# A routed expert stage whose TensorE program is written out slot by slot, in place of a hardware loop

## The chip, the cores and the metric

The kernel runs on one core of a Trainium2 chip. The metric is the device time of one execution in microseconds (us). A core has five engines with instruction streams of their own: TensorE (PE: matmuls, with the weight loads shown as PEld), VectorE (DVE), ScalarE (ACT), GpSimd (POOL) and SyncE (SP). They meet through semaphores. Sixteen DMA engines move data between HBM and SBUF.

## The reference

Three blocks over 4096 rows (2 sequences of 2048) of 256 numbers, all in fp32. The middle block is a state space layer; the first and the last are the same feed-forward layer with a shared expert and eight routed ones:

```python
x = x + 0.5 * ffn(layernorm(x), ...)
x = x + attn(layernorm(x), ...)      # x @ W_in, causal conv, 16-state recurrence, silu, @ W_out
x = x + 0.5 * ffn(layernorm(x), ...) # the same weights as the first

def swiglu(x, wg, wu, wd):
    return silu(x @ wg.T) * (x @ wu.T) @ wd.T

def ffn(h, gate_w, shared_gate, shared_up, shared_down, r_gate, r_up, r_down):
    shared_out = swiglu(h, shared_gate, shared_up, shared_down)
    logits = h @ gate_w.T
    top_id = argmax(logits, axis=-1)
    xs = h * sigmoid(max(logits, axis=-1))[:, None]
    routed_out = 0
    for e in range(8):
        xe = where((top_id == e)[:, None], xs, 0.0)
        routed_out += swiglu(xe, r_gate[e], r_up[e], r_down[e])
    return shared_out + routed_out
```

## The kernel before

**Layout.** fp32 matmuls are made of three passes over operands that are split into a high and a low part (`mm3`, lines 350 to 352: high by high, low by high, high by low). The feed-forward layer is in the program twice, called layer 0 (first block) and layer 1 (third block). Each has this order on TensorE: the shared expert on the first half of the rows, then the routed stage, then the shared expert on the second half.

**Routed stage.** The rows are scattered by expert into `xs_sorted` in HBM, in 39 slots of 128 rows (32 tiles, and up to 7 more since each expert's rows end on a slot's edge). The slots are worked in order, in 13 rounds of `RING` = 3. Which expert a slot belongs to is known only when the kernel runs: DVE writes it into the table `slot_e`, and TensorE reads one entry into a register (`expert_of`, line 537; `TENSOR_LOAD` in the trace). The register's lowest bit picks one of two places of the expert's weights, `wr_hi` and `wr_lo`.

**One slot on TensorE** (`routed_run`, from line 540): 12 matmuls for gate and up of slot s (`m_gate_up`, columns 512), the read of the next slot's expert, 2 transposes of the rows of slot s + 1 (`m_transpose`, line 501), 12 matmuls for down of slot s - 1 (`m_down`, columns 256), and 4 transposes of the hidden rows of slot s (`m_transpose_h`, line 532). ACT and DVE take the results over in between, and SP loads and stores slots (`slot_load`, line 1618; `slot_store`, line 1622).

**Pieces.** `routed_run` is called in pieces. Layer by layer, slots 0 to 2 are written out; a hardware loop of 3 turns holds the code of 9 slots (slots 3 to 11, 12 to 20, 21 to 29); slots 30 to 38 are written out again. Every piece but the first begins with two reads of the table, one for the slot before it and one for its first slot, because nothing is carried over from the piece before. Inside a piece only the following slot is read, in mid-slot. In the loop, the slot number and the semaphore values that are waited for are computed in registers. ACT, DVE and SP have loops of their own over rounds of 3 slots.

**Weights.** POOL loads each expert's weights twice, into `wr_raw` (line 1452) and `wr_hi` (line 1455), 1536 KB each, and subtracts one from the other into `wr_lo` (line 1471, 6.8 us). It starts the load of `wr_hi` of an expert when TensorE has finished the slots of the expert two before it, and that of `wr_raw` as soon as the subtraction before is done.

Of the kernel before, what the change touches and what calls it, by code (L numbers as in the profile page):

```python
# [30 lines left out]
def build(nc, x, w_routed, w_shared, gate_w, w_in, w_out, vecs, b_in, b_out, ssm_a, ssm_bc, ssm_d, out):  # L31
# [19 lines left out]
    NS = NT + E - 1  # L51
    RING = 3
# [19 lines left out]
    with ExitStack() as ctx:  # L72
# [283 lines left out]
        def _(pe):  # L356
# [140 lines left out]
            def m_transpose(L, s, j, use):  # L497

                pe.wait_ge(s_xsl[j], 16 * (L * (NS // RING) + use + 1))
                for kb in range(KB):  # L500
                    mm = pe.transpose(MXT[:, kb * P:(kb + 1) * P], rows[:, j, kb * P:(kb + 1) * P],  # L501
                                      ident[:, :])
                mm.then_inc(s_mt, 1)

            def m_gate_up(L, s, e, par):
                q = L * NS + s
                pe.wait_ge(s_wl, e + (L * E + 1))
                pe.wait_ge(s_mxl, q + 1)
                for o, c0, done in ((MG, 0, s_mg), (MU, UP0, s_mu)):
                    for kb in range(KB):  # L510
                        cs = par * W + (c0 + kb * F)
                        wh = wr_hi[:, :, :].rearrange("p a w -> p (a w)")[:, bass.ds(cs, F)]
                        wl = wr_lo[:, :, :].rearrange("p a w -> p (a w)")[:, bass.ds(cs, F)]
                        mm = mm3(pe, o[:, :], xT_hi[:, kb, 0:P], xT_lo[:, kb, 0:P], wh, wl,
                                 start=(kb == 0), stop=(kb == KB - 1))
                    mm.then_inc(done, 1)

            def m_down(L, s, par):
                q = L * NS + s
                pe.wait_ge(s_mhl, q + 1)  # L520
                for fb in range(FB):
                    cs = par * W + (DN0 + fb * H)
                    wh = wr_hi[:, :, :].rearrange("p a w -> p (a w)")[:, bass.ds(cs, H)]
                    wl = wr_lo[:, :, :].rearrange("p a w -> p (a w)")[:, bass.ds(cs, H)]
                    mm = mm3(pe, MY[:, 0:H], hT_hi[:, fb, 0:P], hT_lo[:, fb, 0:P], wh, wl,
                             start=(fb == 0), stop=(fb == FB - 1))
                mm.then_inc(s_slot, 1)

            def m_transpose_h(L, s):
                pe.wait_ge(s_mh, L * NS + s + 1)  # L530
                for fb in range(FB):
                    mm = pe.transpose(MHT[:, fb * P:(fb + 1) * P], hf[:, 0, fb * P:(fb + 1) * P],  # L532
                                      ident[:, :])
                mm.then_inc(s_mth, 1)

            def expert_of(s):
                e = pe.value_load(slot_e[0:1, bass.ds(s, 1)], min_val=0, max_val=E - 1)
                return e, e % 2

            def routed_run(L, i0, count, first=False, last=False):  # L540

                prev = None if first else expert_of(i0 * RING - 1)[1]
                now = expert_of(i0 * RING)
                for a in range(count):
                    for j in range(RING):
                        i, s = i0 + a, (i0 + a) * RING + j
                        end = a == count - 1 and j == RING - 1
                        m_gate_up(L, s, *now)
                        following = None if end else expert_of(s + 1)
                        if not (last and end):  # L550
                            m_transpose(L, s + 1, (j + 1) % RING, i + (j + 1) // RING)
                        if prev is not None:
                            m_down(L, s - 1, prev)
                        m_transpose_h(L, s)
                        prev, now = now[1], following
                if last:
                    m_down(L, (i0 + count) * RING - 1, prev)

            def routed_slots(L):
                pe.wait_ge(s_tab, L + 1)  # L560
                pe.wait_ge(s_add, 2 * (L * NG + NH))
                m_transpose(L, 0, 0, 0)
                routed_run(L, 0, 1, first=True)

                rounds, each = NS // RING - 1, 3
                loops = (rounds - 1) // each
                with pe.Fori(0, loops) as h:
                    routed_run(L, each * h + 1, each)
                routed_run(L, loops * each + 1, rounds - loops * each, last=True)

            def w_in_sums():

# [130 lines left out]
            pe.wait_ge(s_wsl, 1)  # L703
            shared(0, 0)
            routed_slots(0)
            shared(0, 1)
            attention()
            shared(1, 0)
            routed_slots(1)
            shared(1, 1)  # L710

# [1042 lines left out]
```

## Time and profile before

| | us |
|---|---|
| median of 3 runs | 957.38 |
| lowest and highest of them | 955.56, 959.16 |
| the profiled execution, its own time | 956.44 |
| span in its trace | 954.3 |
| TensorE busy, all matmuls | 893.9 |
| routed stage of layer 0, slots 0 to 38 | 153.4 to 355.2 |
| routed stage of layer 1, slots 0 to 38 | 677.8 to 876.5 |

All times in the trace are counted from the start of the span. The profiled execution took 956.44 us, 2.1 us more than its span; it lies 0.9 us under the median. A matmul's end is modelled, and matmuls overlap, so the starts are the safe numbers: the distance from the first gate matmul of one slot to that of the next is the slot's period. Idle time called "issue" is time in which TensorE waited for nothing that the profile shows. Register instructions and branches do not count as busy; they appear under PEldq, TensorE's sequencer.

### The profile page before, as it was taken

Reading aid. Unit: us, or ns where it says so; the run is one execution under the profiler, and the core shown is the slowest. Engines: PE = TensorE matmul, PEld = TensorE weight load, DVE = VectorE, ACT = ScalarE, POOL = GpSimd, SP = SyncE. Lnnn points to the kernel's source line nnn. Section 1 sums busy time; section 2 is a strip of 40 time slices with the busy share of each in tenths; the row PEclk is TensorE's granted clock in tenths of the full one; section 3 lists DMA queues with packets and bytes.
Section 4 is the critical chain, followed back from the end, with each engine's and each line's share of the span. In section 5 each row is a group of like instructions: output and inputs, shape, how many; then the busy total and the mean of one; then the engine's idle time right before and its main releaser. Section 6 shows DMA issues by size and latency. Waiting matters only on the chain.

```text
span 954.3 us, 16363 instructions
## 1 busy us (share of the span) xinstructions
PE 893.9 (94%) x5430; PEld 784.7 (82%) x5431; DVE 476.3 (50%) x1007; ACT 383.2 (40%) x747; POOL 459.1 (48%) x427
## 2 busy tenths in 40 slices
PE   4899998999999999998999997999899999998998
PEld 3788887888888888887989997888788888887887
DVE  6447553333333335558998983755333333333453
ACT  1134232333333333346677765423233333333331
POOL 3314764124242207864999985376431242220883
PEclk9999999999999999999999998799999999999999
DMA  8836564355555316520011104646434555511557
GB/s 279 285 122 235 161 242 166 111 188 177 185 182 180 100 39 149 72 29 1 12 29 29 45 23 143 201 164 244 165 124 177 185 187 176 188 56 57 93 101 182
DMA packets 75676, 130.85 MB, mean 137 GB/s; under 512 B 6650, under 2 KB 67716, under 8 KB 71268
## 3 DMA queue, kind: packets, MB, share of 16 engines
q0 software_dynamic: 18688, 74.33, 25.2%
q1 hardware_dynamic: 56932, 55.75, 18.4%
q8 instruction: 38, 0.62, 0.3%
q14 instruction: 18, 0.15, 0.1%
HBM read 93.74 MB, written 36.32 MB: 136 GB/s over the span
## 4 chain that ended last, share of the span: by engine, by line
PE 70%; DMA 11%; DVE 7%; POOL 5%; issue 4%; ACT 1%; SPq 1%; POOLq 0%; ACTq 0%; DVEq 0%
PE bank L350 19%; PE bank L352 18%; PE bank L351 18%; DMA rows<-xs_sorted 9%; PE bank L425 4%; PE bank L417 3%; PE bank L532 3%; PE bank L501 2%; DMA xs_sorted<-rows,pos 1%; DVE v L1164 1%; POOL v L1410 1%; POOL xs_sorted L1438 1%; DMA rows<-xn_kept 1%; POOL hT_lo L1414 1%; DVE xT_lo L945 1%
## 5 line engine op out<-in xcount | busy, mean ns | idle before, releaser
L350 PE MATMUL bank<-wr_hi,xT_hi 128*128 x312 | 130.4, 418 | 9.9 <-issue 7.5
L1471 POOL TENSOR_TENSOR wr_lo<-wr_raw,wr_hi 128x3072 fp32r<-128x3072 f32 x14 | 95.1, 6795 | 87.0 <-DMA wr_hi<-w_routed 86.9
L1495 POOL DMA_INDIRECT acc<-ys_sorted,pos x64 | 102.2, 1597 | 62.4 <-DMA ys_sorted<-rows 41.2
L352 PE MATMUL bank<-wr_lo,xT_hi 128*128 x312 | 123.9, 397 | 0.0
L351 PE MATMUL bank<-wr_hi,xT_lo 128*128 x312 | 123.7, 396 | 0.0
L1121 DVE TENSOR_TENSOR hf<-sg,bank 128x512 f32<-128x512 f32 x78 | 53.6, 687 | 135.7 <-PE bank L352 135.7
L945 DVE TENSOR_TENSOR hT_lo<-bank,hT_hi 128x512 fp32r<-128x512 f32 x78 | 54.0, 692 | 125.7 <-ACT hT_hi L716 125.7
L350 PE MATMUL bank<-xT_hi,ws_hi 128*128 128x512 f32 x256 | 102.3, 400 | 3.9 <-DVE xT_lo L945 2.7
L351 PE MATMUL bank<-xT_hi,ws_lo 128*128 128x512 f32 x256 | 101.6, 397 | 0.0
L716 ACT ACTIVATE xT_hi<-bank 128x256 fp32r<-128x256 f32 (+1 forms) x126 | 56.0, 463 | 112.8 <-PE bank L501 96.0
L352 PE MATMUL bank<-xT_lo,ws_hi 128*128 128x512 f32 x256 | 101.2, 395 | 0.0
L732 ACT ACTIVATE sg<-bank 128x512 f32<-128x512 f32 x64 | 38.3, 598 | 154.4 <-PE bank L352 154.3
L350 PE MATMUL bank<-wr_hi,hT_hi 128*128 x312 | 94.3, 302 | 3.0 <-DVE hT_lo L945 3.0
L352 PE MATMUL bank<-wr_lo,hT_hi 128*128 x312 | 88.1, 282 | 0.0
L351 PE MATMUL bank<-wr_hi,hT_lo 128*128 x312 | 87.8, 281 | 0.0
L1043 DVE TENSOR_TENSOR hf<-sg,bank 128x512 f32<-128x512 f32 x64 | 43.8, 687 | 76.5 <-PE bank L352 76.2
L1438 POOL DMA_INDIRECT xs_sorted<-rows,pos x64 | 64.8, 1013 | 35.7 <-DVE rows L1083 17.9
L350 PEld LDWEIGHTS bank<-wr_hi,xT_hi 128*128 128x128 f32 x312 | 59.3, 190 | 23.0 <-issue 12.4
L780 ACT ACTIVATE sg<-bank 128x512 f32<-128x512 f32 x78 | 46.6, 597 | 77.0 <-PE bank L352 77.0
L1164 DVE SCALAR_TENSOR_TENSOR v<-bank,vec,v 128x511 f32<-128x511 f32 (+2 forms) x96 | 71.0, 747 | 7.5 <-ACT v L849 5.0
L1455 POOL DMA_DIRECT2D wr_hi<-w_routed x16 | 8.9, 555 | 136.0 <-PE bank L352 136.0
L350 PE MATMUL bank<-ws_hi,hT_hi 128*128 128x256 f32 x256 | 73.5, 287 | 0.0
(236 smaller groups left out, 2265.2 us busy)
## 6 DMA issues: line engine op xcount, KB each, us to landing
wr_raw<-w_routed POOLq DMA_DIRECT2D x16, 1536.0 KB, 7.0
wr_hi<-w_routed POOLq DMA_DIRECT2D x16, 1536.0 KB, 7.8
rows<-xs_sorted SPq DMA_DIRECT2D x78, 128.0 KB, 2.4
ys_sorted<-rows SPq DMA_DIRECT2D x78, 128.0 KB, 1.7
xn_kept<-xg SPq DMA_DIRECT2D x16, 512.0 KB, 3.3
xg<-xn_kept SPq DMA_DIRECT2D x16, 512.0 KB, 4.3
rows<-xn_kept SPq DMA_DIRECT2D x16, 512.0 KB, 4.1
acc<-x SPq DMA_DIRECT2D x8, 512.0 KB, 7.4
```

The lines of the kernel that those rows point to most:

```text
L350: pe.matmul(o, a_hi, b_hi, start=start, stop=False, skip_group_check=True)
L351: pe.matmul(o, a_lo, b_hi, start=False, stop=False, skip_group_check=True)
L352: return pe.matmul(o, a_hi, b_lo, start=False, stop=stop, skip_group_check=True)
L716: return act.activation(o, i, ACT.Copy)
L780: act.activation(sg[:, 0, :], MG[:, :], ACT.Silu).then_inc(s_msg, 1)
L945: return dve.tensor_tensor(o, full, f32(h), ALU.subtract)
L1043: dve.tensor_tensor(hf[:, fb % 2, :], sg[:, fb % 2, :], U2[fb % 2][:, :], ALU.mult).then_inc(s_h, 1)
L1121: dve.tensor_tensor(hf[:, 0, :], sg[:, 0, :], MU[:, :], ALU.mult).then_inc(s_mh, 1)
L1164: dve.scalar_tensor_tensor(vb_[:, d:GN], UB[cb % 2][:, 0:GN - d], vec[:, cb, k:k + 1], vb_[:, d:GN], ALU.mult, ALU.add).then_inc(s_tap if ...
L1438: pool.indirect_dma_start(out=xs_dram, out_offset=bass.IndirectOffsetOnAxis(ap=pos[:, tt:tt + 1], axis=0), in_=rows[:, half * GT + t, :], ...
L1471: pool.tensor_tensor(wr_lo[:, e % 2, :], wr_raw[:, :], f32(wr_hi[:, e % 2, :]), ALU.subtract).then_inc(s_wl, 1)
L1495: pool.indirect_dma_start(out=acc[:, tt, :], out_offset=None, in_=ys_dram, in_offset=bass.IndirectOffsetOnAxis(ap=pos[:, tt:tt + 1], axis= ...
```

## The change

On TensorE, the four pieces of the routed stage (three calls of `routed_run`, one of them in a loop) become one call that writes out all 39 slots. The table is read once for each slot, and what was read is carried on. All slot numbers and semaphore values are constants. The order of matmuls and of what they wait for is unchanged. The other engines' programs are the same. TensorE's program grows from 4476 to 6032 rows (both layers, waits left out, a matmul with its weight load as one row).

```diff
@@ -560,13 +560,7 @@
                 pe.wait_ge(s_tab, L + 1)
                 pe.wait_ge(s_add, 2 * (L * NG + NH))
                 m_transpose(L, 0, 0, 0)
-                routed_run(L, 0, 1, first=True)
-
-                rounds, each = NS // RING - 1, 3
-                loops = (rounds - 1) // each
-                with pe.Fori(0, loops) as h:
-                    routed_run(L, each * h + 1, each)
-                routed_run(L, loops * each + 1, rounds - loops * each, last=True)
+                routed_run(L, 0, NS // RING, first=True, last=True)
 
             def w_in_sums():
```

The places that move are the seams between the pieces: one where the loop is entered (between slots 2 and 3), two where it returns, one where it is left (between slots 29 and 30), in each layer. L567 is the line of the loop, `slot_e` the table, `m_h_done` the semaphore of the hidden rows. Here is TensorE's program before, in layer 0, from the last transposes of slot 2 to the first wait of slot 3:

```order
L532 MATMUL bank<-ident,hf 128x128 [waits m_h_done]
L532 MATMUL bank<-ident,hf 128x128 x3
L567 UNCONDITIONAL_BRANCH
L567 ISA
L537 REGISTER_ALU
L537 TENSOR_LOAD slot_e
L537 ISA x3
L537 TENSOR_LOAD slot_e
L537 ISA x2
L507 REGISTER_ALU
L508 REGISTER_ALU [waits wr_lo_done]
L350 ISA [waits m_xT_lo_done]
```

In the changed kernel the same place, and every other edge between slots, reads so:

```order
L532 MATMUL bank<-ident,hf 128x128 [waits m_h_done]
L532 MATMUL bank<-ident,hf 128x128 x3
L507 REGISTER_ALU
L350 ISA [waits m_xT_lo_done,wr_lo_done]
L350 MATMUL bank<-wr_hi,xT_hi 128x512
```

The branch, both reads and their register work are gone from between the transposes and the next slot's first matmul. The second place is the end of the loop's code in layer 0 and the start of the written-out slots 30 to 38, before:

```order
L532 MATMUL bank<-ident,hf 128x128 [waits m_h_done]
L532 MATMUL bank<-ident,hf 128x128 x3
L567 REGISTER_ALU
L567 COMPARE_AND_BRANCH
L537 TENSOR_LOAD slot_e
L537 ISA x2
L537 TENSOR_LOAD slot_e
L537 ISA x2
L507 REGISTER_ALU
L350 ISA [waits m_xT_lo_done,wr_lo_done]
```

In the changed kernel this place too has the five rows of the fence above it. One read stays for each slot; it stands in mid-slot, behind the twelve gate and up matmuls, as it does inside the pieces before.

## Rows read from the trace of the kernel before

**Rows 1.** The page: the chain that ended last, shares of the span by engine
```profile
PE 70%; DMA 11%; DVE 7%; POOL 5%; issue 4%; ACT 1%; SPq 1%; POOLq 0%; ACTq 0%; DVEq 0%
```

**Rows 2.** Nine slots each: length, busy PE, PEld, DVE, ACT, POOL, PE clock, DMA
```profile
170.30:216.81 46.51, 44.52 (x271) 38.54 (x271) 15.84 (x28) 17.49 (x36) 11.94 (x5) 1.00 0.45 154
...
263.39:309.81 46.42, 44.56 (x270) 38.56 (x271) 15.20 (x27) 17.44 (x36) 15.22 (x7) 1.00 0.54 186
309.81:353.60 43.79, 43.78 (x268) 38.54 (x268) 15.09 (x26) 16.54 (x35) 5.44 (x4) 1.00 0.23 73
```

**Rows 3.** Timeline of TensorE: start, duration, instruction, idle time before it
```profile
174.84 0.60 PE L532 MATMUL bank<-ident,hf 128*128 128x128 f32 x4
175.19 0.48 PE L350 MATMUL bank<-wr_hi,xT_hi 128*128 x1
...
215.12 0.60 PE L532 MATMUL bank<-ident,hf 128*128 128x128 f32 x4
216.81 0.49 PE L350 MATMUL bank<-wr_hi,xT_hi 128*128 x1 [1.09 <-issue]
```

**Rows 4.** TensorE's waits, 160:352.5, then 682:874: total us, times, longest
```profile
PE bank L350 <- issue: 3.6, 4, 1.1
PE bank L501 <- DMA rows<-xs_sorted: 3.1, 6, 0.7
...
PE bank L350 <- issue: 3.9, 4, 1.1
PE bank L501 <- DMA rows<-xs_sorted: 0.9, 2, 0.5
```

**Rows 5.** TensorE's sequencer, lines 537 and 567: count, ns min/median/max
```profile
L537 PEldq TENSOR_LOAD <-slot_e x86: 296/302/498, 151.8 to 865.8; - x86
...
L567 PEldq COMPARE_BRANCH  x6: 83/218/235, 214.5 to 829.2; - x6
```

**Rows 6.** The chain of waits: start, us, a slot load behind a weight load
```profile
181.14 7.28 DMA rows<-xs_sorted
```

**Rows 7.** Timeline of POOL and TensorE around the last weight load of layer 1
```profile
825.60 0.55 POOL L1455 DMA_DIRECT2D wr_hi<-w_routed  x1 [9.48 <-PE bank L352]
833.28 6.80 POOL L1471 TENSOR_TENSOR wr_lo<-wr_raw,wr_hi 128x3072 fp32r<-128x3072 f32 x1 [7.13 <-DMA wr_hi<-w_routed]
...
831.15 0.49 PE L350 MATMUL bank<-wr_hi,xT_hi 128*128 x1 [0.83 <-issue]
...
834.05 0.38 PE L501 MATMUL bank<-ident,rows 128*128 128x128 f32 x2
```

**Rows 8.** Timeline of POOL: weight loads in layer 0, then in layer 1
```profile
220.43 0.55 POOL L1452 DMA_DIRECT2D wr_raw<-w_routed  x1 [0.30 <-POOL wr_lo L1471]
226.99 0.55 POOL L1455 DMA_DIRECT2D wr_hi<-w_routed  x1 [6.01 <-PE bank L352]
...
769.55 0.57 POOL L1452 DMA_DIRECT2D wr_raw<-w_routed  x1 [0.30 <-POOL wr_lo L1471]
774.84 0.55 POOL L1455 DMA_DIRECT2D wr_hi<-w_routed  x1 [4.72 <-PE bank L352]
```

**Rows 9.** DMA queues, packets, MB, share: 180.5:188.5, 216:310 (whole list), 310:356, whole span
```profile
q8 instruction: 1, 0.02, 0.9%
...
q0 software_dynamic: 1152, 12.58, 37.1%
q1 hardware_dynamic: 5184, 4.72, 15.7%
...
q8 instruction: 3, 0.05, 0.4%
...
q8 instruction: 38, 0.62, 0.3%
```

**Rows 10.** Slot 0 of layer 0 and of layer 1, columns as in rows 2
```profile
153.40:159.43 6.03, 5.40 (x18) 4.00 (x19) 1.02 (x2) 0.98 (x2) 0.83 (x2) 0.72 0.77 268
677.82:682.30 4.48, 3.85 (x18) 2.88 (x19) 1.02 (x2) 0.98 (x2) 1.38 (x2) 1.00 0.56 163
```

## The prediction, made before the changed kernel was run

> **What bounds the kernel now.** I began with the chain that ended last. TensorE holds 70% of it, and "issue", time in which nothing that the profile shows was waited for, holds 4% [rows 1]. So a gap on TensorE is worth its length, if what waits behind it moves along. Next came the stretches of nine slots in the routed stage of layer 0, cut at the edges of the pieces. The reader is to compare the length with the busy PE: the first and the third turn of the loop take 46.51 and 46.42 us, and the written-out slots 30 to 38 take 43.79 us for the same matmuls, with TensorE busy for 43.78 [rows 2]. 43.79 / 9 = 4.87 us is thus a slot's period with no gap, and a turn of the loop loses 2.6 to 2.7 us.
>
> The timeline shows where. Between two slots inside a piece the last transposes start at 174.84 and the next slot's first matmul at 175.19: 0.35 us, which is 0.25 less than the modelled 0.60 of the transposes. At a return of the loop the same two starts are 215.12 and 216.81, 1.69 us apart, with 1.09 us of idle "issue" between [rows 3]. So a seam costs its idle time and 0.25 us more: 1.69 - 0.35 = 1.34 = 1.09 + 0.25. The waits of TensorE give all of them: 4 idle times "issue" of 3.6 us in layer 0 and 4 of 3.9 us in layer 1 [rows 4], one for each seam and none elsewhere between slots. The other idle time in the stage is before the transposes of the next slot's rows, on the load of `rows` from `xs_sorted`: 3.1 us in 6 places and 0.9 us in 2 [rows 4]. It is not touched by the edit.
>
> ACT, DVE and SP return from loops of their own at every third slot. If those were the cause, the gap would stand at every third slot; it stands at the four seams only.
>
> **What the change removes.** At each seam TensorE's sequencer has the loop's branch, two reads of the table and register work to do after it has issued four short transposes, and only their 0.60 us of work covers that. A read takes 302 ns in the middle of 86, a compare and branch 218 ns in the middle of 6 [rows 5]. Two reads and a branch are 0.82 us, and register work takes the rest of what is seen. In mid-slot the same read is covered by the backlog of twelve matmuls in front of it, and costs nothing in slots 30 to 38: busy 43.78 of 43.79 [rows 2]. After the change each edge is of that kind, and the number of reads falls from 86 to 78.
>
> Sum: layer 0 loses 3.6 + 4 x 0.25 = 4.6 us, layer 1 loses 3.9 + 4 x 0.25 = 4.9 us. Together **9.5 us less**.
>
> Register arithmetic inside the loop's slots goes too. A bound on what it costs now: a turn is 46.5 us at most, less 43.8, less a seam of at most 1.34, less its share of the slot load waits (3.1 idle and 6 x 0.17 of overlap lost, over three turns, 1.4): nothing or 0.1 us a turn, under 0.5 us in both layers. I take zero, since it lies before matmuls that are already queued, and the lower end is zero as well.
>
> **What the change adds.** First, program text. 18 slots a layer that were turns of the loop are now fetched. In the 94 us from 216 to 310, inside the loop, the list of DMA queues has no instruction queue at all; in the 46 us of the written-out slots 30 to 38 and a little more it has 3 packets of 16 KB [rows 9]. At 2 to 3 packets for nine slots, 18 slots in each of two layers add 8 to 12 packets to the 38 of the whole execution. Their price in a straight line: the stretch with 3 packets has no gap, and the 8 us from 180.5, under a weight load, have one such packet and no idle "issue". I take zero; the upper end is the rival on code below.
>
> Second, **given back on slot loads**. A slot's rows are loaded one to two slots before they are transposed. Where such a load is issued right behind a weight load it takes 7.28 us [rows 6], and TensorE waits a little for it. Eleven of the twelve weight loads `wr_hi` have no seam between the issue of the slot load and its use, so their waits stay what they are. The twelfth has one. It is issued at 825.60 and the subtraction that waits for it starts at 833.28; the slot load behind it lands about then. TensorE uses those rows at 834.05, after a seam of 0.83 + 0.25 = 1.08 us [rows 7]. Without the seam it would come at 832.97 and wait until 833.28: **0.3 us** given back.
>
> Third, the weights. POOL loads `wr_raw` at a fixed distance behind its own work, and `wr_hi` when TensorE has finished an expert. Where a seam lies between, the distance shrinks. It is 226.99 - 220.43 = 6.56 us in one of two such places of layer 0, and becomes 5.2. Layer 1 has already a distance of 774.84 - 769.55 = 5.29 us [rows 8] with no longer wait after it. POOL's idle time before these loads, 6.01 and 4.72 us [rows 8], is also about how early the next expert's weights are ready; minus 1.34 it stays above 3 us, so TensorE does not start to wait for `wr_lo`. A slot load behind `wr_raw` may lose some tenths where it comes 1.3 us nearer to it: 0 to 0.3 us in each of three places. I take 0.1 us in all.
>
> So 9.5 - 0.3 - 0.1 = **9.1 us** less. What follows each stage (the shared expert's second half, the gathers, the attention block) starts from it and moves along whole: none of it has a fixed time of its own. The span becomes 954.3 - 9.1 = 945.2, the profiled execution 956.44 - 9.1 = 947.3. It lay 0.9 under the median, and the forecast goes by the median: 957.38 - 9.1 = **948.3 us**.
>
> **What the skill says of a seam.** In this trace a return costs 1.34 us, and no instruction packet is moved from 216 to 310, though the loop returns in there. The Trainium skill, in "Runtime: NRT & Kernel Launch", section "Instruction fetch mechanics", says that a taken branch whose target isn't in the current two-page window forces a fetch before work goes on; no run of before shows such a fetch at a return. By that rule the seam would be a fetch, and by the rows it is sequencer work; the sum is the same, as both go. The Trainium skill, in "Advanced Engine Details and Errata", section "Control Flow Timing", gives about 51 ns for a branch and 108 ns for a compare and branch; the trace has 218 ns for most of the latter. By that page alone the loop itself would be worth under 1 us over eight seams, an estimate, and the reads would have to be the rest.
>
> **The rivals.** (1) *Slot loads take part of the gain.* They are the only other idle time in the stage, and a faster TensorE needs them sooner. The longest wait now is 0.7 us [rows 4]. If all twelve loads behind a weight load came to wait so long, that is 8.4 us in place of the present 4.0: 4.4 us given back, 957.38 - 9.5 + 4.4 = 952.3 us. Against it: eleven are triggered by TensorE itself and keep their distance. Chance 0.08.
>
> (2) *The idle time is not the seam's.* Something at a slot's start that the trace doesn't name could hold it, as the register work in front of the first matmul, and the edge of a written-out slot could keep most of it. Then under 1 us changes, about 956.5 us. Against it: slots 31 to 38 have these very edges and no gap [rows 2]. Chance 0.04.
>
> (3) *Slower: code comes late.* The loop ran from code already on chip, and the new text is fetched in the same 94 us in which weights take 37.1% of the DMA engines' time [rows 9]. Suppose a packet is asked for only when it is needed. Of 10 added packets four would queue behind weights for up to the 7.3 us of a slot load there, and six cost about 1.3 us, the dearest seam as the nearest row for an unloaded fetch: 4 x 7.3 + 6 x 1.3 = 37 us, 985 us. It decides from 0.9 us a packet, where the gain is gone. Against it stand the packets in straight code that cost nothing, one of them under weights. Chance 0.04.
>
> Besides, TensorE's clock in slot 0 is 0.72 in layer 0 (part of it at 1.2 GHz) and 1.00 in layer 1, after a short idle time in both, and the slot takes 6.03 against 4.48 us [rows 10]. The two could change places or both go one way: 1.6 us up or down, whatever the change does.
>
> **How the numbers follow.** The forecast has 0.84. Around 948.3 lie the clock's 1.6 us, 0.5 for register work, 0.9 more for loads behind `wr_raw`, and the spread of the runs (1.8 us on either side of the median): 945.3 to 951.6. To leave out no more than 2 in 10, the upper end goes to rival (1): **945.0 to 952.5 us**. A measurement of this kernel can tell about 0.5% from no change, 4.8 us: faster means below 952.6. Faster 0.84 and most of (1)'s 0.08: 0.90. Within 0.5%: the rest of (1) and (2): 0.06. Slower 0.04.
>
> **What would show it.** Right: no idle "issue" before L350 between slots; 78 reads and no compare and branch; layer 0's stage down from 201.8 us by 4.6, layer 1's from 198.7 by 4.5; 46 to 50 instruction packets, some of them in the stretch that had none; slot load waits near 4 us in all with a new one of 0.3 in slot 30 of layer 1. Wrong: idle "issue" spread over the written-out slots at any place (code), the load waits of [rows 4] grown to 8 us (rival 1), or a gap left at every slot's start (rival 2).

## The result, and the profile of the changed kernel

The changed kernel takes **960.03 us** (median of 16 runs, 958.01 to 965.39), the kernel before 957.39 us on the same chip (16 runs). The ratio is **1.0032, 95% interval 1.0019 to 1.0046**: no change by the bound of 0.5%, and if anything 0.3% slower. The forecast was 948.3 us. The profiled execution took 960.17 us, with a span of 958.1 us; that is 3.8 us more than the span before. Of all the runs below one execution, the profiled one of e14_clean_after (999.87 us at a granted clock of 0.85), was in a slower state, and what is said of that kernel goes by its four others.

The page of the changed kernel: the chain by engine, the instruction queue, and the group of gate matmuls with the idle time before them.

```profile
PE 63%; DMA 16%; POOL 8%; DVE 6%; issue 4%; ACT 1%; SPq 1%; POOLq 0%; ACTq 0%; DVEq 0%
...
q8 instruction: 49, 0.80, 0.3%
...
L350 PE MATMUL bank<-wr_hi,xT_hi 128*128 x312 | 131.0, 420 | 2.4 <-DVE xT_lo L939 2.4
```

Two things can be read. The gate matmuls have no idle "issue" in front of them any more: the eight seams of [rows 4] are gone. And the chain has 16% DMA, where it had 11% [rows 1]. So the gain was made and then spent, and DMA is where to look.

The waits of TensorE (us in total, times, longest), in layer 0's stage (160 to 356), in layer 1's (682 to 880), and in the 80 us ahead of layer 1's (600 to 682):

```profile
PE bank L501 <- DMA rows<-xs_sorted: 4.6, 6, 2.0
...
PE bank L501 <- DMA rows<-xs_sorted: 5.8, 7, 1.9
...
PE bank L501 <- DMA rows<-xs_sorted: 3.2, 1, 3.2
PE bank L350 <- DVE hT_lo L939: 2.6, 1, 2.6
```

The first two rows answer to [rows 4], 3.1 and 0.9 us. Idle time alone understates them, as at the seams. By the starts of the matmuls on both sides, the waits for slot loads cost 4.1 us in layer 0 and 2.1 in layer 1 before, and 5.6 and 7.6 after.

**Where 3.8 us come from.** The start of the same matmul in both traces, the changed kernel's minus the first one's:

| place in the program | time before | changed, minus before |
|---|---|---|
| first shared tile before layer 0's stage | 126.9 | -0.1 |
| end of layer 0's stage | 356.7 | -3.1 |
| end of the attention block | 599.0 | -3.4 |
| inside layer 1's first half, a few us ahead of the last row load | 651.9 | -3.5 |
| slot 0 of layer 1 | 677.8 | +1.6 |
| end of layer 1's stage | 878.1 | +3.8 |

Layer 0 gains 3.1 of the 4.6 us that were forecast; 1.5 go to slot loads. Layer 1's stage should gain 4.9 and loses 2.2. Just before it 5.1 us go, where nothing was changed. In numbers: -9.5 for the seams, +1.5 in layer 0, -0.4 in between, +5.1 at the entry of layer 1's stage, +1.3 for the clock in its slot 0, and the rest, +5.8, in its slot loads (7.6 - 2.1 = 5.5 by their own count): 3.8.

The slow loads, from the chain of waits (start, us), two in layer 1 and one in layer 0; [rows 6] has 7.28 for such a load:

```profile
296.13 8.48 DMA rows<-xs_sorted
...
777.31 8.54 DMA rows<-xs_sorted
...
828.99 8.65 DMA rows<-xs_sorted
```

In the timeline around the first of them, POOL waits for the weights (8.84 us in the bracket) and TensorE for the slot's rows:

```profile
304.55 6.80 POOL L1465 TENSOR_TENSOR wr_lo<-wr_raw,wr_hi 128x3072 fp32r<-128x3072 f32 x1 [8.84 <-DMA wr_hi<-w_routed]
...
304.66 0.44 PE L501 MATMUL bank<-ident,rows 128*128 128x128 f32 x2 [2.01 <-DMA rows<-xs_sorted]
```

The same load of weights in the kernel before:

```profile
306.84 6.78 POOL L1471 TENSOR_TENSOR wr_lo<-wr_raw,wr_hi 128x3072 fp32r<-128x3072 f32 x1 [7.57 <-DMA wr_hi<-w_routed]
```

The slot load stands behind the weight load, so 1.27 us more for the weights (8.84 - 7.57) are about as much more for the rows (8.48, and 7.18 at this place before). Before, all twelve loads of `wr_hi` had POOL waiting 6.9 to 7.6 us; after, nine have 7.0 to 7.6 and three 8.66, 8.79 and 8.84.

Three further waits of the changed kernel are new: at 273.2, 753.7 and 801.1, worth 0.90, 0.88 and 0.54 us by the starts. They stand behind the other weight load, `wr_raw`. With the seam gone, SP issues the slot load some 1.3 us nearer to it. The first of them, from POOL's timeline and from the chain:

```profile
264.52 0.55 POOL L1446 DMA_DIRECT2D wr_raw<-w_routed  x1 [0.30 <-POOL wr_lo L1465]
...
265.91 7.25 DMA rows<-xs_sorted
```

Before, the same three slot loads were issued 2.6 to 2.7 us behind `wr_raw`, took 4.8 to 5.0 us, and TensorE did not wait for them. After, they come 1.3 to 1.4 us behind it and take 6.9 to 7.3. So of the 7.0 us that slot loads cost more, about 5 are at the three slow loads of `wr_hi` (0.3 of it forecast) and 2.3 here, while some others are a little shorter.

**The entry.** From the chain of the changed kernel, ahead of layer 1's stage: the last scatter of a group of rows, then the load of the last group's rows (`rows<-xn_kept`), which SP issues when that scatter has landed.

```profile
649.59 4.14 DMA xs_sorted<-rows,pos
653.74 13.87 DMA rows<-xn_kept
```

And POOL's timeline there, the two weight loads of expert 1, after the change and then before:

```profile
653.49 0.59 POOL L1446 DMA_DIRECT2D wr_raw<-w_routed  x1 [0.30 <-POOL wr_lo L1457]
654.08 0.59 POOL L1449 DMA_DIRECT2D wr_hi<-w_routed  x1
...
657.02 0.59 POOL L1452 DMA_DIRECT2D wr_raw<-w_routed  x1 [0.30 <-POOL wr_lo L1463]
657.61 0.59 POOL L1455 DMA_DIRECT2D wr_hi<-w_routed  x1
```

Before, SP issued that row load at 655.8, 1.2 us ahead of `wr_raw`, and it landed in 4.0 us. After, it is issued at 653.74, 0.25 us behind `wr_raw`, and takes 13.87 us beside 3 MB of weights. DVE, POOL's scatters, slot 0's rows and TensorE wait for it in turn. `wr_raw` is issued 3.90 us behind the issue of the last scatter in both kernels. The race is lost because that scatter took 4.14 us to land, and 2.7 before.

What made the scatter late can be read too. These are the DMA rows between its issue and its landing, after the change and then before; the change has an instruction packet there:

```profile
q8 instruction: 1, 0.02, 1.9%
xs_sorted<-rows,pos POOLq DMA_INDIRECT x1, 4.1
...
xs_sorted<-rows,pos POOLq DMA_INDIRECT x1, 2.7
```

The scatter's semaphore is raised once by each of sixteen parts. In the changed kernel fifteen of them have landed by 2.75 us, as before, and the sixteenth lands at 4.14, 2.4 us after the packet's start at 1.7. The experiments below have this again and again.

**What was forecast of the profile and is there.** The reads of the table, and what the queues moved from 213 to 307, the stretch in which [rows 9] had no instruction queue:

```profile
L537 PEldq TENSOR_LOAD <-slot_e x78: 296/301/497, 151.9 to 869.4; - x78
...
q0 software_dynamic: 1152, 12.58, 38.1%
q1 hardware_dynamic: 5184, 4.72, 15.8%
q8 instruction: 6, 0.10, 0.4%
```

78 reads, no loop line, 49 instruction packets (46 to 50 were forecast), six of them inside the stretch that had none.

### The profile page after: what moved, and what is told of

It is laid out like the page before. It is cut to its first block, busy times and chain, and to the rows that moved or that the text cites. A ratio compares the mean times of both kernels' runs of the same rounds, so it can differ in the third digit from the quotient of the medians.

```text
span 958.1 us, 16225 instructions
## 1 busy us (share of the span) xinstructions
PE 893.8 (93%) x5430; PEld 785.1 (82%) x5430; DVE 477.3 (50%) x1007; ACT 383.3 (40%) x747; POOL 459.0 (48%) x427
## 3 DMA queue, kind: packets, MB, share of 16 engines
q1 hardware_dynamic: 56932, 55.75, 18.4%
## 4 chain that ended last, share of the span: by engine, by line
PE 63%; DMA 16%; POOL 8%; DVE 6%; issue 4%; ACT 1%; SPq 1%; POOLq 0%; ACTq 0%; DVEq 0%
PE bank L350 17%; PE bank L352 17%; PE bank L351 17%; DMA rows<-xs_sorted 11%; PE bank L425 4%; PE bank L417 3%; PE bank L532 2%; POOL v L1404 2%; DMA rows<-xn_kept 2%; PE bank L501 2%; DMA xs_sorted<-rows,pos 2%; POOL hT_lo L1408 2%; POOL xs_sorted L1432 1%; DVE v L1158 1%; DVE rows L1077 1%
## 5 line engine op out<-in xcount | busy, mean ns | idle before, releaser
L939 DVE TENSOR_TENSOR xT_lo<-bank,xT_hi 128x256 fp32r<-128x256 f32 (+1 forms) x126 | 63.5, 520 | 25.1 <-ACT xT_hi L710 24.8
L351 PE MATMUL bank<-ws_hi,hT_lo 128*128 128x256 f32 x256 | 72.5, 283 | 0.0
```

The costliest lines, as they stand in the source:

```text
L351: pe.matmul(o, a_lo, b_hi, start=False, stop=False, skip_group_check=True)
L939: return dve.tensor_tensor(o, full, f32(h), ALU.subtract)
```

## Experiments

Ratios are to the kernel before in runs on the same chip, with 95% intervals. "Lead" is the time by which the last row load is issued ahead of `wr_raw` at layer 1's entry; before it is 1.2 us. Letters for theories are those of the texts on record.

### Is it the seam, or the text that is fetched?

**e1_one_turn** keeps the loop and lets its one turn hold 33 slots: two seams a layer stay, and nearly the same text is fetched as after the change.

```diff
-                rounds, each = NS // RING - 1, 3
+                rounds, each = NS // RING - 1, 11
```

> The kernel before, with a loop of one turn of 33 slots in place of three turns of 9: in each layer two seams (entered, left) in place of four, and as much program text to fetch as in the changed kernel. Theory C (the fetched text gives the gain back, since its packets make slot loads behind weight loads 1.5 us longer): as the changed kernel plus 4 seams of 1.2 us, about 965 us, 46 to 50 instruction packets, and some of the 12 weight loads of wr_hi at 8.7 us in place of 7.2. Theory P (the gain is lost by where TensorE stands against the weight loads, text is free): 4 seams fewer than before, 952 to 956 us, no weight load over 7.7 us.

Measured 956.79 us, ratio 0.9974 (0.9956 to 0.9992). Its page has 49 packets too. TensorE's waits in layer 0's and layer 1's stage:

```profile
PE bank L501 <- DMA rows<-xs_sorted: 2.6, 5, 1.2
PE bank L350 <- DVE hT_lo L945: 1.5, 1, 1.5
PE bank L350 <- issue: 1.2, 2, 0.7
...
PE bank L501 <- DMA rows<-xs_sorted: 3.8, 5, 1.8
PE bank L350 <- issue: 1.3, 2, 0.8
```

Two of the four seams are left in each layer. Fetched text leaves no gap of its own on TensorE. Neither theory came out whole. The 965 us of C did not come, but two of its slow `wr_hi` loads did, 8.10 us in layer 0 and 8.72 in layer 1, where P allowed 7.7 at most. 956.8 lies just above P's 952 to 956. The lead was 0.1 us, and nothing was lost at the entry.

**e2_reads_kept** has no loop, but the pieces and their two reads at each seam.

```diff
-                routed_run(L, 0, NS // RING, first=True, last=True)
+                routed_run(L, 0, 1, first=True)
+                for h in range(3):
+                    routed_run(L, 3 * h + 1, 3)
+                routed_run(L, 10, 3, last=True)
```

> The changed kernel, written out without a loop, but in the four pieces of before, so that each seam keeps its two reads of the table and loses only the branch. Two reads and their register work are 0.6 to 1.0 us of a seam. The seams' idle time should be 0.5 to 0.9 us each in place of 0.6 to 1.1. Theory C: text is fetched as in the changed kernel, 960 + 8 x 0.8 = 966 us. Theory P: seams hold TensorE nearly where it stood before, so the loads meet as before, 955 to 957 us.

Measured 956.47 us, ratio 0.9977 (0.9961 to 0.9993). TensorE's waits in layer 0's stage:

```profile
PE bank L501 <- DMA rows<-xs_sorted: 3.3, 5, 1.2
PE bank L350 <- issue: 1.5, 4, 0.4
```

Four idle times are left, but of 1.5 us in place of 3.6 [rows 4]. Over both layers each is 0.33 to 0.50 us, where the text on record had 0.5 to 0.9. By the starts a seam now costs 0.58 to 0.75 us, where one with the loop costs 0.84 to 1.34 in the kernel before. So the two reads are 0.6 to 0.7 us of it, and branch and loop registers the other half us. The kernel as a whole gained less than the removed halves (some 4 us), with one `wr_hi` wait of 8.04.

### The slot loads

**e3_early_after** is the changed kernel with one edit on SP: the load of slot s + 4 is issued ahead of the wait for the result of slot s; in the original it comes a slot later, behind that wait. **e4_early_before** is the same edit in the kernel before.

```diff
-                with sp.Fori(0, NS // RING - 1) as i:
+                sp.wait_ge(s_mt, L * NS + 1)
+                slot_load(L, RING, 0)
+                with sp.Fori(0, NS // RING - 2) as i:
                     for j in range(RING):
                         s = i * RING + j
-                        sp.wait_ge(s_mt, L * NS + s + 1)
-                        slot_load(L, s + RING, j)
+                        sp.wait_ge(s_mt, L * NS + s + 2)
+                        slot_load(L, s + RING + 1, (j + 1) % RING)
                         slot_store(L, s, j)
```

> The changed kernel, with SP issuing the load of each slot one slot earlier: ahead of the wait for the result that it stores, no longer behind it. If the gain went into waits on slot loads (both theories say so), those waits go, 4.6 us of idle time in layer 0 and 5.8 in layer 1, and 2 us more of overlap: about 948 us. If something else took the gain, the time stays at 958 to 960.

> The kernel before with the same earlier slot loads. Its waits on slot loads are 4.0 us idle, about 6 with the lost overlap: 951 to 952 us. With the run of the changed kernel in the same form it gives the worth of the seams once slot loads can't be late: 9.5 us if the forecast's term was right.

Measured: e3 948.61 us, ratio 0.9877 (0.9852 to 0.9903); e4 952.32 us, ratio 0.993 (0.9916 to 0.9945). TensorE's waits in e3, layer 0's stage and then layer 1's, have no slot load left. What is late next are weights, by tenths:

```profile
PE bank L350 <- DVE hT_lo L939: 1.5, 1, 1.5
...
PE bank L350 <- DVE xT_lo L939: 1.6, 1, 1.6
PE bank L350 <- DVE hT_lo L939: 1.5, 1, 1.5
PE bank L350 <- POOL wr_lo L1465: 0.5, 1, 0.5
```

The stages from slot 0 to slot 38, e3 and then e4, columns as in [rows 2]:

```profile
153.93:340.66 186.73, 186.10 (x1128) 162.96 (x1129) 64.47 (x113) 72.72 (x150) 49.10 (x21) 0.99 0.47 158
676.21:863.16 186.95, 185.82 (x1128) 162.89 (x1129) 64.48 (x113) 72.72 (x150) 48.75 (x19) 0.99 0.45 152
...
154.19:346.60 192.41, 188.02 (x1129) 163.54 (x1129) 64.56 (x113) 72.89 (x150) 48.77 (x21) 0.98 0.45 153
677.06:867.28 190.22, 185.46 (x1129) 161.80 (x1129) 64.47 (x113) 72.90 (x150) 48.46 (x19) 1.00 0.44 149
```

The two stages' slots 0 differ in clock. Against the 4.87 us of a later slot, theirs took 1.17 and 1.13 us more in e3, and 2.23 more and 0.38 less in e4, whose layer 1 ran it at full clock. Without that the edit is worth 5.68 - 1.06 = 4.6 us in layer 0 and 3.27 + 1.51 = 4.8 in layer 1: the 4.6 and 4.9 of the forecast. This is the test of its main term. Three loads of `wr_hi` took over 8.6 us in layer 0 here, and cost nothing.

But e3 is only 3.7 us faster than e4. Its chain at the entry says why:

```profile
646.08 4.70 DMA xs_sorted<-rows,pos
...
650.80 13.28 DMA rows<-xn_kept
```

`wr_raw` was issued at 650.00, 0.8 us earlier than the row load. (Its last scatter took 4.70 us, again with an instruction packet under it.) TensorE was 7.0 us ahead of the kernel before at 652 and 1.6 us ahead at slot 0: 5.4 lost. In e4 the lead was 1.3 us and nothing was lost.

### The entry of layer 1

**e5_row_first** is the changed kernel with a wait on POOL until the last row load has landed, before expert 1's weights are asked for. **e6_both_after** has this and the early slot loads, **e7_both_before** both edits in the kernel before.

```diff
                     if g == 5:
+                        pool.wait_ge(s_rl[1], 16 * (L * (NG // 2) + NG // 2))
                         load_expert(L, 1)
```

> The changed kernel, with one wait more on POOL ahead of the two loads of expert 1's weights in each layer: until the rows of the last scatter group have landed. POOL is idle there for 2.5 us anyway. In the changed kernel the load of these rows is issued 0.2 us behind the weights (653.7 against 653.5) and takes 13.9 us in place of 4.0, and TensorE enters layer 1's routed stage 5.1 us later than it should; in the kernel before it is 1.2 us ahead of them. Theory R (this race took the 5 us): the load takes 4 to 5 us again, the time from the last group's transposes at 648 to the first slot is 24.4 us from the transposes, as before, and the time is 5 us under the changed kernel's, 954 to 956. If the race is an accident of one profile, the time stays at 960.

> The changed kernel with both: slot loads issued one slot earlier, and the rows of the last group ahead of the weights. With no slot load late and no race, the whole worth of the seams should arrive: about 5 us under the changed kernel with early slot loads alone, 943 to 944 us.

> The kernel before with both. The rows of its last group are ahead of the weights already, so the second edit should do nothing: as the kernel before with early slot loads alone, 952 us. The difference to the changed kernel with both is the worth of eight seams, 9.5 us by the forecast's term; under 6 us would say that the term itself was too large.

Measured: e5 960.21 us, ratio 1.0017 (0.9997 to 1.0037); e6 949.88, ratio 0.9902 (0.9884 to 0.9919); e7 957.53, ratio 0.9979 (0.9964 to 0.9993). None gained; 954 to 956, 943 to 944 and 952 had been expected. POOL's timeline in e5:

```profile
659.61 0.59 POOL L1447 DMA_DIRECT2D wr_raw<-w_routed  x1 [5.34 <-DMA rows<-xn_kept]
```

The row load was quick, and the entry lost 2.5 us in place of 5.1. But the weights came 5 us later, on top of the last scatters and the first slot loads: slots 5 and 6 of layer 1 took 2.9 and 1.1 us longer than 4.87, with a `wr_hi` wait of 8.94. The wait moved the collision. The entry itself still lost 3.9 us in e6. In e7 it cost some 5 us against e4, where there had been nothing to cure. With both edits the change is worth 957.53 - 949.88 = 7.6 us.

**e12_weights_apart** asks for the same 3 MB in two parts and at other times: `wr_hi` of expert 1 behind the scatters of group 2, `wr_raw` in the old place. Early slot loads are in. **e13_clean_before** is the same in the kernel before, **e14_clean_after** is e12 again beside it, **e15_apart_after** has the weights apart without the early slot loads, **e16_clean_reads** has e2's reads at the seams with both.

```diff
+                    if g == 2:
+                        pool.dma_start(wr_hi[:, 1, :], w_routed[1, :, :]).then_inc(s_wh, 16)
                     if g == 5:
-                        load_expert(L, 1)
+                        pool.wait_ge(s_wl, L * E + 1)
+                        pool.dma_start(wr_raw[:, :], w_routed[1, :, :]).then_inc(s_wraw, 16)
```

> The changed kernel with early slot loads, and with the two weight loads of expert 1 taken apart: wr_hi is issued behind the scatter of group 2, wr_raw stays behind group 5. The last row load then meets 1.5 MB in front of it in place of 3. If the entry to layer 1's routed stage is late because of this meeting, it comes back: the row load takes 7 us at most in place of 13.3, the entry gains 3 to 5 us, 944 to 946 us against 948.6. If the earlier weights only delay other row loads, it stays at 948 or more.

> The kernel before with slot loads one slot earlier and expert 1's weight loads taken apart. It has all its seams. Theory G (the seams' worth was right, 9.5 us, and was lost at the slot loads and at the entry): it is 9 to 10 us slower than the changed kernel in the same form, about 954 against 945. If the difference is under 6 us, the term itself was too large or a third place takes it.

> The changed kernel with the same two edits, on the same chip as the one above: 945 us, as e12. In its trace: no wait on a slot load inside the stages, no idle time called issue between slots, the entry to layer 1 without the 3 us wait.

> The changed kernel with expert 1's weight loads taken apart, slot loads as they are. It gains what the entry to layer 1's routed stage lost: 4 to 6 us, 954 to 956 us. If it stays at 960, the entry is not worth what the trace says, since later waits absorb it.

> The clean form, written out in the four pieces of before: the branch is gone, the two reads at each seam stay. By the trace a read is 0.30 us and a seam 1.2: with two reads and their register work hidden only by four transposes, a seam keeps 0.6 us, so 8 x 0.6 = 4.8 us over the clean changed kernel, about 950. If the branch were all of the price, it equals that kernel.

| kernel | us | ratio, 95% interval |
|---|---|---|
| e12_weights_apart | 945.24 | 0.984, 0.9814 to 0.9867 |
| e13_clean_before | 952.40 | 0.9934, 0.9915 to 0.9954 |
| e14_clean_after (four runs) | 944.72 | 0.9855, 0.9832 to 0.9878 |
| e15_apart_after | 953.71 | 0.9975, 0.995 to 1.0 |
| e16_clean_reads | 948.21 | 0.9914, 0.9886 to 0.9942 |

e12 is the fastest version, 1.4 to 1.6% below the kernel before. In it the entry loses nothing (5.6 us ahead at 652, 5.7 at slot 0). Its stages, and then those of e13:

```profile
153.79:340.89 187.10, 186.25 (x1129) 162.83 (x1129) 64.47 (x113) 72.74 (x150) 49.44 (x22) 0.99 0.47 158
672.17:859.10 186.93, 185.84 (x1129) 162.79 (x1129) 64.47 (x113) 72.72 (x150) 48.36 (x19) 0.99 0.45 152
...
155.17:346.34 191.17, 186.66 (x1128) 163.00 (x1129) 64.49 (x113) 72.93 (x150) 49.32 (x22) 0.99 0.45 154
676.04:866.19 190.15, 185.46 (x1129) 161.78 (x1129) 64.48 (x113) 72.90 (x150) 48.38 (x19) 1.00 0.44 149
```

The difference is 4.1 and 3.2 us; with layer 1's slot 0 at equal clock (1.14 above 4.87 us in e12, 0.40 under it in e13) the second is 4.8: 8.8 us in both. Whole kernels differ by 952.40 - 944.72 = 7.7 us on one chip. The trace is e12's, which is the same kernel as e14.

e16 lies 3.5 us above e14 (4.8 had been expected) and 4.2 below e13: reads and loop share the seam, as in e2, with an uncertainty of some 2 us either way.

e15 tells the two losses apart. TensorE's waits in its two stages:

```profile
PE bank L501 <- DMA rows<-xs_sorted: 2.7, 4, 1.0
...
PE bank L501 <- DMA rows<-xs_sorted: 2.6, 5, 0.7
```

The entry lost nothing, and the `wr_hi` waits were 7.5 us at most but for one of 7.92. Slot loads cost 3.8 and 3.9 us by the starts, where the changed kernel had 5.6 and 7.6 with three slow loads. By its ratio, against 1.0032 and 1.0011 (e11, below) of the changed kernel, it is 3.5 to 5.5 us faster: about the entry's 5.1.

### Does fetched text slow the weights?

**e8_extra_packets** is the kernel before, and SP moves 16 KB from HBM to HBM once a round of three slots.

```diff
+                        if j == 1:
+                            sp.wait_ge(s_extra, 16 * (L * (NS // RING) + i + 1))
+                            extra_load()
                         slot_load(L, s + RING, j)
```

> The kernel before, with SP moving 16 KB from HBM to HBM once in each round of three slots, about as often as the changed kernel fetches program text, and ahead of a slot load. Theory C (such traffic makes loads behind the weights late): two to four of the 12 waits for wr_hi at 8 us or more in place of 7.6 at most, slot load waits up by 3 to 6 us, 960 to 963 us. Theory P: 958 us or less, the waits as before.

Measured 959.99 us, ratio 1.0009 (0.9993 to 1.0025). Its queues of data and instructions:

```profile
q1 hardware_dynamic: 57764, 56.18, 18.4%
q8 instruction: 38, 0.62, 0.3%
```

832 packets more than the 56932 of the kernel before, 32 for each of 26 transfers: they are cut and spread, and so no image of one 16 KB packet. Eleven loads of `wr_hi` waited 6.8 to 7.7 us and one 8.17. Extra bytes at this rate don't do it. Whether one large packet among a load's sixteen parts does was not imitated.

**e9_layer0_only** and **e10_layer1_only** write the stage out in one layer and keep the loop in the other (`if L == 0:` or `if L == 1:` around the two forms).

> The change in layer 0 alone; layer 1 keeps its loop. Every straight-text kernel so far had the last wr_hi load of layer 0 (at about 295) waited for 8.0 to 8.8 us where kernels with the loop have 7.2 to 7.6, and most had the same in layer 1 (at about 828). Theory F (text fetched at that time does it): layer 0's last wait is over 8, layer 1's under 7.5. Theory T (the mere size of the program, or where its data then lies, does it): both over 8. Time: layer 0 gives 3 us, and layer 1's entry either loses 5 us (if the race of the row load comes from the shift of time) or not (if it comes from the text of layer 1): 959 or 954.

> The change in layer 1 alone; layer 0 keeps its loop. Theory F: layer 0's last wait for wr_hi under 7.6, layer 1's over 8. Theory T: both over 8. Up to layer 1 the program is that of before, so the entry to its routed stage should be as before if the race comes from a shift in time, and 2 to 5 us late if it comes from text. Time 955 to 958.

Measured: e9 961.1 us, ratio 1.0018 (0.9998 to 1.0039); e10 954.71, ratio 0.9961 (0.9943 to 0.9979). Both have 43 instruction packets. The slow loads are in the layer that is written out, and only there: 8.07 and 8.41 us in e9's layer 0, all at most 7.31 in its layer 1; 8.05 and 8.06 in e10's layer 1, all at most 7.56 in its layer 0. One of them in e10:

```profile
781.57 6.81 POOL L1474 TENSOR_TENSOR wr_lo<-wr_raw,wr_hi 128x3072 fp32r<-128x3072 f32 x1 [8.06 <-DMA wr_hi<-w_routed]
```

So the length of the whole program is not the cause. Theory F is met in its layers, but not in its place: e10's last load waited 7.21 us, and the two over 8 us are earlier loads (8.05 and 8.06 us). Nor does the text on record hold for every kernel without a loop; e6's last load of layer 0 had 7.29. The entry race follows layer 0: e10 kept the loop there, its lead was 1.3 us and nothing was lost, e9 lost 6.1 us. Its chain:

```profile
650.31 4.46 DMA xs_sorted<-rows,pos
654.78 14.34 DMA rows<-xn_kept
```

Thus half of the change alone (layer 1) is 0.4% faster, and the other half alone is as slow as both.

**e11_after_again** is the changed kernel once more.

> The changed kernel once more, for a second profile. If the three places where it lost its gain are of the kernel and not of one execution, then again: slot load waits of 10 to 14 us in the two stages against 6 before, the last wr_hi wait of each layer over 8 us, and layer 1's first slot 4 to 6 us late against the last transposes of the shared stage. The slow first matmuls of layer 1 (1.3 us, half clock) may come or not.

Measured 960.18 us, ratio 1.0011 (0.999 to 1.0033). It loses 4.9 us at the entry again, and its slot 0 of layer 1 takes 6.04 us where the kernel before has 4.48. Slot loads cost 9.7 us by the starts, just under the 10 to 14 on record. Only one `wr_hi` wait is over 8 us here (8.96, the last). The entry is the steady loss, the slow loads vary in number and place.

**All traces together.** Of the loads of `wr_hi` inside a stage that is written out, or is one turn long, 27 of 132 kept POOL waiting 8 us or more; inside a stage with the loop 4 of 72. Those four stand at one place, expert 5 of layer 1, where `wr_raw` is issued only 5.3 us ahead of it [rows 8]. Without that place it is 22 of 121 against 0 of 66. That is an association of kernels. (e14 is left out here.)

The traces allow a closer look, load by load. The semaphore of a `wr_hi` load is raised by sixteen parts, and in 19 of the 204 loads the last part landed 1.0 us or more behind the fifteenth. All three slow loads of the changed kernel are of this kind: fifteen parts landed by 7.2 to 7.5 us as usual, the last at 9.1 to 9.2. In 16 of the 19 an instruction packet began between 0.5 us ahead of the load's issue and 7 us behind it, and so it did in 56 of the 185 others. So a packet is often there when one part is late, and often does nothing. The other slow loads, as in layer 0 of e3 and e12, have several parts late and partly no packet; their cause is open.

**The last scatter before the race** is the clearest case. With no instruction packet between its issue and its landing it took 2.62 to 2.68 us (before, e4, e7, e8, e10). With one it took 3.60 to 4.71 (the changed kernel, e1, e2, e3, e5, e6, e9, e11). In each of these eight traces fifteen parts had landed by 2.75 us, and only the sixteenth came later, 2.4 to 2.8 us after the packet's start. In e12 to e16, where a weight load is ahead of it, the picture is less clean: 3.24 us without a packet (e13), 2.80 to 3.40 with one (e12, e15, e16).

It is the text of layer 0 that puts the packet there. In the five traces with the three-turn loop in layer 0 the nearest packet began 6.4 to 7.4 us ahead of this scatter; in the eight, with layer 0's text fetched in full, one began 1.1 to 2.1 us behind its issue. No experiment moved a packet by itself.

## Why the prediction was wrong, point by point

- **What bounds the kernel, and what a seam costs: right.** Eight seams, 9.5 us. With slot loads and entry out of the way the stages measure 9.4 (e3 against e4) and 8.8 (e12 against e13) of it, and whole kernels 7.7 (e14 against e13), with a slower clock in layer 1's slot 0 on the changed side of e12's trace (6.01 us against 4.48).
- **Split of the seam: right in kind.** Two reads take some 0.6 us and the loop's part 0.5 to 0.6 in e2, where the text had 0.60 for the reads, and 0.22 and register work for the rest. The Trainium skill, in "Advanced Engine Details and Errata", section "Control Flow Timing", gives 51 and 108 ns for branches; in e2 the branch with the loop's registers is worth some five times the latter.
- **Register work inside the slots: right at zero.** Slots of either form without a wait have a period of 4.87 us.
- **Code fetch: right in number and in its price on TensorE, wrong in what it left out.** 49 packets, and no "issue" idle between slots. Rival 3 (985 us) did not come. But the text asked only whether TensorE waits for a packet, not what a packet does to the transfers beside it: one part of sixteen late by 1.0 to 2.1 us in the scatter before the race.
- **"Given back on slot loads", 0.3 + 0.1 us: the term that was mis-sized.** It measured 1.5 us in layer 0 and 5.5 in layer 1. The reasoning was that eleven of twelve loads keep their distance to TensorE. That took the 7.28 us of [rows 6] as a constant. Where TensorE waits already [rows 4] there is no slack, so each us that a weight load takes longer comes out on TensorE: the three waits of about 2 us follow the three slow loads. The 0.1 us for loads behind `wr_raw` had the right mechanism and the right number of places, and the distance to the next weight load shrank as forecast (5.26 us for 5.2); but it measured 2.3 us, since 1.3 us less distance made those slot loads 2.1 to 2.5 us longer. Rival 1 had the mechanism, but was bounded by 0.7 us a wait and 8.4 in all; the sum was 5.6 + 7.6 = 13.2 us.
- **The 0.3 us itself** was at the right place. In e11 and e1 the last load of layer 1 cost most of all, 2.25 and 1.98 us.
- **"What follows moves along whole": failed.** This is the larger error in the part that came again in every profile of the change: 5.1 us here, 4.9 in e11, 6.1 in e9, and 5.4 in e3. The claim was argued from the fact that nothing there has a fixed time. It does hold for the attention block (3.1 us ahead at 357, 3.4 at 599). It missed that layer 1's first half has a race between two queues, SP's row load and POOL's weights, decided by 1.2 us, on a scatter that lands after 2.6 to 2.7 us, or after 3.6 to 4.7 where an instruction packet falls on it. No row of it was read ahead of the prediction.
- **Weights late for TensorE: right.** No wait for `wr_lo` in the changed kernel; 0.4 to 0.7 us came up in the stages only when slot loads were early (e3, e6, e12, e16).
- **The clock** fell on the bad side: 1.3 us in layer 1's slot 0 (5.83 us against 4.48), inside the 1.6 that was allowed for. The row of this slot, columns as in [rows 2], has a granted clock of 0.75, where [rows 10] has 1.00:

```profile
679.42:685.25 5.83, 5.20 (x19) 3.91 (x19) 1.02 (x2) 0.98 (x2) 2.07 (x2) 0.75 0.55 174
```

The longer idle time ahead of it (3.2 and 2.6 us in the waits above) is not shown to be the cause. e9 had waits of 3.4 and 1.9 us there and took 4.49 us for the slot; e8, e12, e15 and e16 had 0.8 us and took 6.0 to 6.2.

- **The rivals.** Rival 1 capped the loss at 4.4 us, and none spoke of the entry. The chance of 0.84 rested on counting the work that was removed, and the range had no room for what the faster stage would collide with. Its four terms, added plainly, span 944.4 to 952.6 us; the text does not say how they became 945.3 to 951.6, and the measured 960.03 lies outside either.

**What stays open.** Why an instruction packet makes one part of a transfer late in some loads and not in others, and what makes several parts late in the rest of the slow loads. That the packet is the cause is read from the traces; an experiment that moves one packet and nothing else was not made.

## What to carry to other kernels

Removing sequencer work from a tight loop is worth what its starts say only if the next thing needed has slack; look for every wait of some tenths on a DMA and ask what it would be if that DMA took 1.5 us longer, and for every load that would be issued nearer behind a large one. A change in the length of the program text also moves every later fetch; compare where the instruction packets fall with the transfers that something waits for. Where a faster stage is followed by transfers from two queues that meet within a microsecond or two, read that place before the sum is made: with the slot loads early and the large transfer asked for in two parts, the same change was worth -0.8% (e14 against e13), where it had measured +0.3%. Making the large transfer wait instead only moved the collision (e5, e7).

## What the runs showed of the hardware

A 512 KB row load that is issued within a microsecond behind a 1.5 MB weight load, with a second such load 0.6 us after the first, takes 13.3 to 14.3 us, and 4.0 us when it is issued 1.2 us ahead of it. Even 0.1 us ahead was enough in e1. The 128 rows of a slot, behind one weight load, take about 7.2 us and up to 8.65 when that load is slow; 2.6 to 2.7 us behind a `wr_raw` load they took 4.8 to 5.2 us, and 1.3 to 1.4 us behind it 6.0 to 7.3. A 16 KB instruction packet that was moved during a scatter went with one of its sixteen parts landing 1.0 to 2.1 us late, in the eight traces of eight that have this with no weight load beside it. A seam of a hardware loop on TensorE with two table reads costs 0.8 to 1.4 us, and 0.58 to 0.76 with the reads alone; the Trainium skill's rule in "Runtime: NRT & Kernel Launch", section "Instruction fetch mechanics", that a taken branch forces a fetch when its target is outside the current two-page window, is not seen. The loop of nine slots returned with no instruction packet from 216 to 310 [rows 9], though 36 more written-out slots took 11 more packets of 16 KB, so that nine slots are some 44 KB of text, an estimate, and the loop's start lies more than two such pages back.
